# Two mixture-of-experts layers: every expert on all rows, against blocks of 256 chosen rows

## The chip, the cores and the metric

The kernel runs on one core of one Trainium2 chip. The metric is device microseconds from launch to the last store. Three runs of the kernel before gave 1663.55, 1663.65 and 1663.83 us; the median is 1663.65 us.

## The reference

The input is `x` of 8 sequences of 256 tokens, 256 features each: 2048 rows. Four sublayers follow, each with a residual and a layer norm. All arithmetic is float32.

```python
x = layernorm(x + attention(x))          # 16 heads of 128, causal, 8 sequences
x = layernorm(x + experts0(x))           # 32 experts of width 96, top 6, shared width 192
x = layernorm(x + state_space(x))        # in_proj, conv, 8 heads of decaying attention, out_proj
x = layernorm(x + experts1(x))           # 16 experts of width 176, top 4 of 2 of 4 groups, shared 352

def experts0(x):
    scores = sigmoid(x @ gate_w)
    topk_w, topk_i = top_k(scores, 6)
    topk_w = topk_w / (sum(topk_w) + 1e-20)
    combine = sum(one_hot(topk_i, 32) * topk_w[..., None], axis=1)     # [t, 32], 6 entries not zero
    act = silu(einsum('td,edf->tef', x, wg)) * einsum('td,edf->tef', x, wu)
    routed = einsum('tef,efd,te->td', act, wd, combine)
    return routed + silu(x @ sg) * (x @ su) @ sd
```

`experts1` is of the same kind, with a softmax, and with four entries of sixteen that are not zero. The reference computes every expert for every row, and multiplies most of the results by zero.

## The kernel before

The instruction stream of each engine is written out by hand, in the order in which it runs; semaphores order the engines against each other. The same `for s in range(...)` loop stands in each engine's block, and each says at which step `s` the engine does what. All matrix products in float32 are three products of rounded halves (`passes`: hi x hi, hi x lo, lo x hi), so each tile that a product reads exists as a high part (written by ScalarE) and a low part (written by VectorE or GpSimd).

**Attention** (lines 547 to 1350 in each engine's `group`) runs over 8 groups of two heads, 16 units each. In its shadow the expert weights are split into halves: SyncE loads a tile of `w_all`, ScalarE (`split_high`) and GpSimd (`split_low`) split it, and SyncE stores it in `w_split`, 56 tiles in all.

**The experts, dense.** The hidden columns of all experts are laid side by side and cut in tiles of 128. A step `s` takes one such tile for one quad (512 rows, a quarter of the tokens): `gate_up(s)` on TensorE makes 12 products of 512 columns (gate and up), ScalarE takes the silu (`gate`, L742), VectorE multiplies (`activate`, L1082), GpSimd multiplies by the combine weights of the rows (`combine`, L578), ScalarE and VectorE make the halves (L750, L1088), and `down(s)`, two steps later, makes 12 products of 256 columns. Layer 0 has 2 shared and 24 expert tiles, layer 1 has 3 and 22, each for 4 quads: 204 steps, 184 of them of experts. Combine weights go through DRAM (`comb_store`, `comb_load`) to be repeated over the partitions.

**The state-space sublayer** works on 4 pairs of sequences (512 rows each). It is not a stage of its own: pair `p` is spread over the steps from `FRONT[p]` on (33, 65, 97, 129), some 50 steps long, so that TensorE does expert tiles between its products. Its head loop goes over 8 heads, 2 steps each: VectorE scans decays (L1152), GpSimd multiplies by `gram` (`mixes`, L600), ScalarE makes the high part (L802), GpSimd the low part (`mix_low`, L606), TensorE the products. The norms and gates of the quads are spread in the same way (`NORM0`, `NORM1`).

## Time and profile before

| | |
|---|---|
| median of three runs | 1663.65 us |
| profiled execution, first to last instruction | 1664.1 us |
| TensorE busy | 1607.4 us (97%) |
| VectorE busy | 1131.1 us (68%) |
| ScalarE busy | 764.6 us (46%) |
| GpSimd busy | 628.7 us (38%) |
| DMA | 277.75 MB, mean 167 GB/s |

The page gives the execution that was profiled by its span, 1664.1 us, which lies 0.45 us above the median of the runs; no other time of it is given. "PE" is TensorE, "DVE" VectorE, "ACT" ScalarE, "POOL" GpSimd, "SP" SyncE, which issues all DMAs of the kernel before. Busy time of TensorE has overlaps in it: the records of two products that follow each other overlap, so the distance of two starts, not the duration, is what a product costs. The first expert product starts at 611.4 us; what is before it is attention, what is behind it are the 204 steps with everything else between them. The last 9 us are the last quad's norm and store.

### The profile page before, as it was taken

The page shows a single profiled execution, that of the slowest core. Times are in us where ns is not written, and L with a number is a line of the kernel's source. Part 1 is how long each engine was busy: PE and PEld are TensorE (multiplying, and loading weights), DVE is VectorE, ACT ScalarE, POOL GpSimd, SP SyncE. Part 2 cuts the span into 40 slices and gives each one's busy share as a digit, 9 for nine tenths or more (in the row PEclk, how much of TensorE's full clock was granted, in tenths as well). Part 3 has the DMA queues.
Part 4 walks back from the last instruction along what each step waited for, and adds up shares of the span by engine and source line. Part 5 has one row for each costly group of instructions (what it writes and reads, how often), then busy time and mean ns, then how long its engine had stood idle before and what let it go on. Part 6 is the DMA issues. An engine that isn't in the chain of part 4 may idle for free.

```text
span 1664.1 us, 29632 instructions
## 1 busy us (share of the span) xinstructions
PE 1607.4 (97%) x9944; PEld 1403.7 (84%) x9944; DVE 1131.1 (68%) x2877; ACT 764.6 (46%) x1889; POOL 628.7 (38%) x379
## 2 busy tenths in 40 slices
PE   7999999999999979999999999999999999999997
PEld 6988888898888868888888888888888888888886
DVE  5878878787887765556467568748784867753533
ACT  5666656666665543434433443325333533323221
POOL 2322223232222004323377335841575147533242
PEclk9999999999999999999999999999999999999999
DMA  6444335343443016666676556655655466555563
GB/s 212 159 140 143 141 118 180 132 158 139 142 141 137 1 59 205 191 196 205 199 225 188 184 176 209 194 187 165 207 189 175 146 206 197 178 175 172 195 206 107
DMA packets 101241, 277.75 MB, mean 167 GB/s; under 512 B 13488, under 2 KB 17584, under 8 KB 100112
## 3 DMA queue, kind: packets, MB, share of 16 engines
q1 hardware_dynamic: 101136, 276.39, 51.6%
q8 instruction: 61, 1.00, 0.2%
q14 instruction: 44, 0.36, 0.1%
HBM read 229.18 MB, written 46.63 MB: 166 GB/s over the span
## 4 chain that ended last, share of the span: by engine, by line
PE 60%; issue 14%; DVE 13%; POOL 6%; ACT 4%; DMA 1%; SPq 1%; POOLq 0%; DVEq 0%; ACTq 0%
PE psum L352 54%; POOL act_sb L578 4%; PE psum L1324 2%; DVE s_sb L1019 1%; PE psum L1335 1%; PE psum L1514 1%; POOL mix L600 1%; ACT p_sb L701 1%; PE psum L1314 1%; ACT kT_hi L660 1%; DVE s_sb L1017 1%; DVE kT_lo L913 1%; DVE pT_lo L1034 1%; DVE x L934 1%; DVE p_sb L1027 1%
## 5 line engine op out<-in xcount | busy, mean ns | idle before, releaser
L352 PE MATMUL psum<-xT_hi,gu_w 128*128 128x512 f32 x1616 | 550.3, 401 | 4.2 <-DVE act_sb L1082 4.0
L578 POOL TENSOR_TENSOR act_sb<-act_sb,comb 128x512 f32<-128x512 f32 x184 | 311.1, 1691 | 614.8 <-DVE act_sb L1082 614.6
L1082 DVE TENSOR_TENSOR act_sb<-psum,gated 128x512 f32<-128x512 f32 x204 | 140.7, 690 | 378.9 <-PE psum L352 372.6
L742 ACT ACTIVATE gated<-psum 128x512 f32<-128x512 f32 x204 | 122.2, 599 | 600.3 <-PE psum L352 597.8
L352 PEld LDWEIGHTS psum<-xT_hi,gu_w 128*128 128x128 f32 x1616 | 304.2, 188 | 78.0 <-DVE act_sb L1082 5.6
L352 PE MATMUL psum<-xT_lo,gu_w 128*128 128x512 f32 x808 | 319.6, 395 | 0.0
L352 PEld LDWEIGHTS psum<-d_w,act_hi 128*128 128x128 f32 x1632 | 221.5, 188 | 19.7 <-issue 2.1
L544 POOL TENSOR_TENSOR split_stage<-raw_stage,split_stage 128x768 fp32r<-128x768 f32 x56 | 103.1, 1840 | 354.2 <-ACT split_stage L650 354.2
L352 PE MATMUL psum<-d_w,act_hi 128*128 128x256 f32 x1632 | 227.7, 282 | 0.4 <-ACT act_hi L750 0.4
L352 PEld LDWEIGHTS psum<-xT_lo,gu_w 128*128 128x128 f32 x808 | 152.2, 188 | 28.8
L1088 DVE TENSOR_TENSOR act_lo<-act_sb,act_hi 128x512 fp32r<-128x512 f32 x204 | 148.8, 729 | 2.1 <-ACT act_hi L750 1.8
L750 ACT ACTIVATE act_hi<-act_sb 128x512 fp32r<-128x512 f32 x204 | 127.3, 624 | 17.1 <-POOL act_sb L578 16.9
L699 ACT ACTIVATE p_sb<-s_sb,neg_max 128x128 f32<-128x128 f32 x128 | 51.5, 403 | 172.0 <-DVE neg_max L1019 172.0
L352 PE MATMUL psum<-d_w,act_lo 128*128 128x256 f32 x816 | 130.1, 282 | 0.0
L352 PE MATMUL psum<-xT_hi,aw_hi 128*128 128x512 f32 x256 | 104.1, 407 | 9.9 <-POOL aw_lo L540 9.9
L352 PEld LDWEIGHTS psum<-d_w,act_lo 128*128 128x128 f32 x816 | 111.2, 188 | 0.0
L352 PE MATMUL psum<-xT_hi,aw_lo 128*128 128x512 f32 x256 | 102.1, 399 | 0.0
L352 PE MATMUL psum<-xT_lo,aw_hi 128*128 128x512 f32 x256 | 101.8, 398 | 0.0
L600 POOL TENSOR_TENSOR mix<-mix,gram 128x768 f32<-128x768 f32 x32 | 94.3, 2947 | 0.0
L1026 DVE TENSOR_SCALAR p_sb<-p_sb,row_inv 128x128 f32<-128x128 f32 x128 | 83.1, 649 | 4.6
L352 PE MATMUL psum<-aw_hi,xT_hi 128*128 128x256 f32 x256 | 74.7, 292 | 9.7 <-DVE kT_lo L913 8.3
L352 PE MATMUL psum<-aw_hi,zT_hi 128*128 128x256 f32 x256 | 80.5, 315 | 2.5 <-DVE zT_lo L1039 2.5
(203 smaller groups left out, 3473.6 us busy)
## 6 DMA issues: line engine op xcount, KB each, us to landing
gu_w<-w_split SPq DMA_DIRECT2D x204, 512.0 KB, 3.6
d_w<-w_split SPq DMA_DIRECT2D x204, 256.0 KB, 3.8
w_split<-split_stage SPq DMA_DIRECT2D x56, 768.0 KB, 3.9
raw_stage<-w_all SPq DMA_DIRECT2D x56, 384.0 KB, 4.3
decay_all<-decay_dram SPq DMA_DIRECT2D x32, 384.0 KB, 5.3
in_w<-w_split SPq DMA_DIRECT2D x40, 256.0 KB, 4.1
aw_raw<-attn_w SPq DMA_DIRECT2D x8, 1024.0 KB, 6.3
comb<-l_comb_dram SPq DMA_DIRECT2D x128, 64.0 KB, 3.1
```

The source lines that it names most:

```text
L352: last = nc.tensor.matmul(out_ap, w, m, start=start and n == 0, stop=stop and n == len(pairs) - 1, **kw)
L544: pool.tensor_tensor(split_stage[:, k % 2, :, 1, :], raw_stage[:, k % 2, :].rearrange("p (j w) -> p j w", j=3), split_stage[:, k % 2, :, 0 ...
L578: pool.tensor_tensor(act_sb[:, s % 2, :], act_sb[:, s % 2, :], comb[:, comb_block(s) % 2, :], ALU.mult).then_inc(comb_done, 1)
L600: pool.tensor_tensor(mix[:, g % MIXES], mix[:, g % MIXES], gram[:], ALU.mult).then_inc(mix_ready, 1)
L660: act.activation(kT_hi[:, bp % 2, j // 2, :], bank, ACT.Copy).then_inc(qkv_hi, 1)
L699: act.activation(p_sb[:, u % 3, 0:P], s_sb[:, u % 2, 0:P], ACT.Exp, bias=neg_max[:, u % 3, 0:1], scale=-1.0, accum_out=row_sum[:, u % 3, 0:1])
L742: act.activation(gated[to, s % 2, :], psum[0:to.stop - to.start, G_BANK, :], ACT.Silu).then_inc(gated_ready, 1)
L750: act.activation(act_hi[rows_of(s), s % 2, :], act_sb[rows_of(s), s % 2, :], ACT.Copy).then_inc(act_hi_ready, 1)
L1026: dve.tensor_scalar(p_sb[:, u % 3, 0:P], p_sb[:, u % 3, 0:P], row_inv[:, u % 3, 0:1], None, ALU.mult)
L1082: dve.tensor_tensor(act_sb[r, s % 2, :], psum[r, G_BANK if packed(s) else U_BANK, :], gated[r, s % 2, :], ALU.mult).then_inc(t_ready, 1)
L1088: dve.tensor_tensor(act_lo[r, s % 2, :], act_sb[r, s % 2, :], act_hi[r, s % 2, :].bitcast(F32), ALU.subtract).then_inc(act_lo_ready, 1)
L1324: last = pe.transpose(psum[:, PT_BANK, i * P:(i + 1) * P], p_sb[:, u % 3, i * P:(i + 1) * P], ident[:])
```

## The change

The expert layers become sparse. `choose` and `slots` on VectorE and `rank` on TensorE (two products with a triangle of ones) number the rows of each expert. For each expert there is a region of 2048 rows in DRAM (`xs`); GpSimd writes each row of `x` into the regions of its 6 (or 4) experts with indirect DMAs, 128 rows of 1 KB each (`scatter`). `table` computes where blocks of 256 rows begin; the number of blocks is fixed by the worst case, 79 in layer 0 and 47 in layer 1, and blocks that no expert needs take rows of zeros. SyncE reads the address of a block from SBUF into a register, loads its rows and its expert's unsplit weights, and stores the block's result in `os`. After the last block GpSimd gathers the 6 (or 4) result rows of each token with indirect DMAs, and VectorE adds them with their weights (`weights`, `combine`).

The state-space sublayer now stands between the two block loops, over slots `t` of its own, with `FRONT` at 14, 46, 78, 110; of the experts only the 12 shared steps of layer 1 are left in it, with the gathers of layer 0 and the scatters of layer 1. In attention 14 tiles are split in place of 56, and SyncE writes zeros to all 42 regions of `xs` (2 MB each).

```diff
 BLOCK = 256
 REGION = T
+def most_blocks(f):
+    return (T * f["top"] + f["experts"] * (BLOCK - 1)) // BLOCK
-SPLITS = 8
+SPLITS = 2
-FRONT = 33, 65, 97, 129
-NORM0 = None, 1, 10, 19
-NORM1 = 28, 54, 82, 115
+FRONT = 14, 46, 78, 110
+SLOTS = FRONT[-1] + 52
+MIX_AT = {t: t if t < QUAD else FRONT[t // QUAD] - 26 + 4 * (t % QUAD) for t in range(TILES)}
+SHARED_AT = {FRONT[p] + 44 + 2 * j: STEPS0 + p * L1["tiles"] + j for p in range(QUADS) for j in range(L1["tiles"])}
...
         @block.sync
+                for k in range(ZEROED):
+                    n = ZEROED * g + k
...
+                    sp.dma_start(dst.rearrange("p (a w) -> p a w", w=1024), zeros[:].to_broadcast([P, REGION // P * D // 1024, 1024])) \
+                        .then_inc(xs_zeroed, 16)
...
+            def first_row_of(n):
+                f, m = block_of(n)
+                return sp.value_load(rows_at[f["layer"]][m:m + 1, 0:1], min_val=0, max_val=f["last_row"])
+            def block_load(n):
+                f, m = block_of(n)
+                row = first_row_of(n)
+                wait(sp, xb_turned, n - XB_RING + 1)
+                sp.dma_start(xb[:, n % XB_RING], xs[bass.ds(row, BLOCK)].rearrange("(i p) d -> p i d", p=P)).then_inc(xb_loaded[n % XB_RING], 16)
+                wait(sp, bw_lo_ready, n - W_RING + 1)
+                sp.dma_start(bw_raw[:, n % W_RING, 0:f["cols"]],
+                             expert_w[f["layer"]][bass.ds(row >> 11, 1)].rearrange("a p w -> p (a w)")).then_inc(bw_loaded[n % W_RING], 16)
+            def block_store(n):
+                _, m = block_of(n)
+                sp.wait_ge(b_copied, n + 1)
+                sp.dma_start(os[m * BLOCK:(m + 1) * BLOCK].rearrange("(i p) d -> p i d", p=P), b_out[:, n % OUT_RING]).then_inc(b_stored[n % OUT_RING], 16)
+            def blocks(f):
+                first = FIRST[f["layer"]]
+                sp.wait_ge(rows_known, f["layer"] + 1)
+                for q in range(QUADS):
+                    sp.wait_ge(scattered[q], 16 * QUAD * (L0["top"] + f["layer"] * L1["top"]))
+                for n in range(first, first + 2):
+                    block_load(n)
+                for n in range(first, first + f["blocks"]):
+                    if n + 2 < first + f["blocks"]:
+                        block_load(n + 2)
+                    if n > first:
+                        block_store(n - 1)
+                block_store(first + f["blocks"] - 1)
...
         @block.gpsimd
-            def combine(s):
-                pool.wait_ge(t_ready, s + 1)
-                pool.wait_ge(comb_loaded[comb_block(s) % 2], comb_landed(comb_block(s)))
-                pool.tensor_tensor(act_sb[:, s % 2, :], act_sb[:, s % 2, :], comb[:, comb_block(s) % 2, :], ALU.mult).then_inc(comb_done, 1)
+            def scatter(f, q):
...
+                pool.wait_ge(placed, QUADS * f["layer"] + q + 1)
+                for t in range(QUAD * q, QUAD * (q + 1)):
+                    for k in range(f["top"]):
+                        pool.indirect_dma_start(xs, bass.IndirectOffsetOnAxis(ap=row_of[:, t, k:k + 1], axis=0), x[:, t, :], None) \
+                            .then_inc(scattered[q], 16)
+            def block_low(n):
...
+                pool.tensor_tensor(bw_lo[:, n % W_RING, w], bw_raw[:, n % W_RING, w], bw_hi[:, n % W_RING, w].bitcast(F32), ALU.subtract).then_inc(bw_lo_ready, 1)
+            def gather(f, t):
+                i = f["layer"] * TILES + t
+                wait(pool, combined, i - MIX_RING + 1)
+                for k in range(f["top"]):
+                    pool.indirect_dma_start(og[:, i % MIX_RING, k, :], None, os,
+                                            bass.IndirectOffsetOnAxis(ap=back_of[f["layer"]][:, t, k:k + 1], axis=0)).then_inc(og_loaded[i % MIX_RING], 16)
...
         @block.tensor
+            def blocks(f):
+                first, end = FIRST[f["layer"]], FIRST[f["layer"]] + f["blocks"]
+                for n in range(first, first + 2):
+                    block_turn(n)
+                block_gate_up(first)
+                for n in range(first, end):
+                    if n + 2 < end:
+                        block_turn(n + 2)
+                    if n + 1 < end:
+                        block_gate_up(n + 1)
+                    block_down(n)
```

`block_turn` makes four transposes of 128x128; `block_gate_up` makes 12 products of 256 columns in layer 0 and 18 in layer 1; `block_down` 6 and 12. Around them ScalarE makes the high parts of the rows (`block_turned`, 512 elements a partition) and of the weights (`block_high`, 640 or 1280), the silu and the high part of the activation; VectorE the low parts, the product and the copy of the result out of PSUM (`block_copy`); GpSimd the low part of the weights (`block_low`).

On GpSimd, just behind attention, before: `combine` of the first expert tiles (`act_sb` is the activation, `comb` the weights of the rows).

```order
L578 TENSOR_TENSOR act_sb<-act_sb,comb 128x512 [waits comb_loaded1,t_ready] x3
L578 TENSOR_TENSOR act_sb<-act_sb,comb 128x512 [waits comb_loaded0,t_ready] x2
L590 TENSOR_TENSOR ow_lo<-ow_raw,ow_hi 128x1024 [waits ow_hi_done]
L578 TENSOR_TENSOR act_sb<-act_sb,comb 128x512 [waits comb_loaded0,t_ready]
L578 TENSOR_TENSOR act_sb<-act_sb,comb 128x512 [waits comb_loaded1,t_ready] x3
```

The same place of the changed kernel, up to the first gathers (`xs` the regions, `row_of` the addresses, `og` the gathered rows, `os` the results):

```order
L674 DMA xs<-x,row_of 86016x256 [waits placed,xs_zeroed]
L674 DMA xs<-x,row_of 86016x256 x23
L700 MEMSET start_row 128x128 [waits o_added]
L702 COPY start_row<-ident 128x128 x2
...
L674 DMA xs<-x,row_of 86016x256 [waits placed]
L674 DMA xs<-x,row_of 86016x256 x23
L681 TENSOR_TENSOR bw_lo<-bw_raw,bw_hi 128x640 [waits bw_hi_ready] x79
L688 DMA og<-os,l_back_of 128x256 [waits weighed,b_stored2,ow_split,b_stored1,b_stored0]
L688 DMA og<-os,l_back_of 128x256 x11
```

The multiplications by the weights are gone from GpSimd's stream, and 96 indirect DMAs stand in it ahead of the first block.

On SyncE's queue, before, the loads of two expert tiles in layer 0:

```order
L439 DMA gu_w<-w_split 128x1024 [waits u_ready]
L444 DMA d_w<-w_split 128x512 [waits down_done]
L460 DMA comb<-l_comb_dram 32x512 [waits comb_stored,comb_done]
L460 DMA comb<-l_comb_dram 32x512 x3
L439 DMA gu_w<-w_split 128x1024 [waits u_ready]
```

After, one block of layer 0 (`xb` its rows, `bw_raw` its weights, `b_out` its result), and the beginning of the next:

```order
L518 TENSOR_LOAD l_rows_at
L518 ISA x2
L524 ISA [waits xb_turned]
L524 DMA xb<-xs 128x2x256
L526 ISA [waits bw_lo_ready]
L526 DMA bw_raw<-l_w 128x640
L532 DMA os<-b_out 128x2x256 [waits b_copied]
L518 TENSOR_LOAD l_rows_at
```

The load of a block's rows now stands behind the store of the block four before it, which waits for its copy out of PSUM.

On GpSimd, in the head loop of pair 1, after (`mix` the decays of a head, `og` the gathers for pair 2, `xs` the scatter of pair 0 for layer 1):

```order
L688 DMA og<-os,l_back_of 128x256 [waits combined]
L688 DMA og<-os,l_back_of 128x256 x5
L711 TENSOR_TENSOR h_lo<-h_tok,h_hi 128x512 [waits h_hi_ready]
L723 TENSOR_TENSOR mix_lo<-mix,mix_hi 128x512 [waits mix_hi_ready]
L717 TENSOR_TENSOR mix<-mix,gram 128x768 [waits gram_copied,since_ready]
...
L674 DMA xs<-x,row_of 86016x256 [waits placed]
L674 DMA xs<-x,row_of 86016x256 x15
L717 TENSOR_TENSOR mix<-mix,gram 128x768 [waits gram_copied,since_ready]
```

Before, an expert's `combine` stands in most of these places; now indirect DMAs do.

## Rows read from the trace of the kernel before

**Rows 1.** The page: busy time by engine, and the chain's shares by engine.

```profile
PE 1607.4 (97%) x9944; PEld 1403.7 (84%) x9944; DVE 1131.1 (68%) x2877; ACT 764.6 (46%) x1889; POOL 628.7 (38%) x379
...
PE 60%; issue 14%; DVE 13%; POOL 6%; ACT 4%; DMA 1%; SPq 1%; POOLq 0%; DVEq 0%; ACTq 0%
```

**Rows 2.** Windows of the span: start:end, length, busy us by engine, clock, DMA share, GB/s.

```profile
300.00:400.00 100.00, 95.61 (x669) 86.16 (x668) 79.36 (x256) 62.61 (x206) 26.26 (x16) 1.00 0.37 130
...
560.00:600.00 40.00, 33.84 (x240) 30.55 (x238) 30.49 (x123) 19.00 (x74) 0.00 (x0) 0.96 0.00 1
...
1000.00:1100.00 100.00, 98.53 (x573) 83.56 (x572) 70.78 (x129) 36.47 (x63) 68.74 (x37) 1.00 0.63 195
```

**Rows 3.** Timeline, 1640 to 1664 us: start us, us, engine, line, operation.

```profile
1643.19 0.60 ACT L742 ACTIVATE gated<-psum 128x512 f32<-128x512 f32 x1 [3.10 <-PE psum L352]
...
1647.43 0.60 ACT L742 ACTIVATE gated<-psum 128x512 f32<-128x512 f32 x1 [3.12 <-PE psum L352]
...
1648.63 1.11 PE L352 MATMUL psum<-d_w,act_hi 128*128 128x256 f32 x8
...
1649.58 0.63 PE L352 MATMUL psum<-d_w,act_lo 128*128 128x256 f32 x4
...
1655.09 1.40 DVE L920 BATCH_NORM_STATS2 stats<-x 128x6 f32<-128x256 f32 x4
...
1659.33 1.38 DVE L934 TENSOR_SCALAR x<-x,mv,rstd 128x256 f32<-128x256 f32 x4
```

**Rows 4.** The chain of waits, 540 to 620 us: start us, us, what.

```profile
591.62 0.87 PE psum L1357 x8
...
611.40 5.19 PE psum L352 x18
```

**Rows 5.** Windows of 5 us around the end of attention.

```profile
585.00:590.00 5.00, 3.96 (x21) 3.99 (x22) 3.76 (x14) 2.18 (x9) 0.00 (x0) 0.66 0.00 0
...
605.00:610.00 5.00, 2.34 (x17) 1.93 (x16) 3.71 (x21) 2.37 (x4) 0.00 (x0) 1.00 0.00 0
610.00:615.00 5.00, 4.63 (x16) 3.66 (x17) 1.57 (x3) 0.60 (x1) 0.00 (x0) 0.66 0.09 21
...
625.00:630.00 5.00, 5.00 (x29) 4.09 (x28) 4.41 (x12) 1.32 (x3) 1.67 (x1) 1.00 0.89 302
```

**Rows 6.** Timeline of SyncE's queue, 1000 to 1012 us.

```profile
1006.90 0.35 SPq L439 DMA_DIRECT2D gu_w<-w_split  x1
```

**Rows 7.** DMA issues of the page: KB each, median us from issue to landing.

```profile
gu_w<-w_split SPq DMA_DIRECT2D x204, 512.0 KB, 3.6
d_w<-w_split SPq DMA_DIRECT2D x204, 256.0 KB, 3.8
...
aw_raw<-attn_w SPq DMA_DIRECT2D x8, 1024.0 KB, 6.3
```

**Rows 8.** Groups of GpSimd over the whole span: mean ns of one behind the busy us.

```profile
L600 POOL TENSOR_TENSOR mix<-mix,gram 128x768 f32<-128x768 f32 x32 | 94.3, 2947 | 0.0
L606 POOL TENSOR_TENSOR mix_lo<-mix,mix_hi 128x512 fp32r<-128x512 f32 x32 | 49.3, 1540 | 11.5 <-ACT mix_hi L802 11.5
...
L590 POOL TENSOR_TENSOR ow_lo<-ow_raw,ow_hi 128x1024 fp32r<-128x1024 f32 x1 | 2.4, 2394 | 0.0
```

**Rows 9.** Groups of VectorE and ScalarE by form, 600 to 1664 us.

```profile
L1088 DVE TENSOR_TENSOR act_lo<-act_sb,act_hi 128x512 fp32r<-128x512 f32 x200 | 146.0, 730 | 2.0 <-ACT act_hi L750 1.8
...
L750 ACT ACTIVATE act_hi<-act_sb 128x512 fp32r<-128x512 f32 x200 | 124.8, 624 | 17.0 <-POOL act_sb L578 16.9
...
L1152 DVE TENSOR_TENSOR_SCAN mix<-decay_all,start_row 128x768 f32<-128x768 f32 x32 | 82.5, 2579 | 0.1
...
L1129 DVE SCALAR_TENSOR_TENSOR conv<-psum,cols,conv 128x508 f32<-128x508 f32 x20 | 14.9, 747 | 0.7
```

**Rows 10.** Timeline of GpSimd, 780 to 960 us, two of the eight mixes of a pair.

```profile
853.87 3.29 POOL L600 TENSOR_TENSOR mix<-mix,gram 128x768 f32<-128x768 f32 x1
...
861.58 1.85 POOL L600 TENSOR_TENSOR mix<-mix,gram 128x768 f32<-128x768 f32 x1
```

985 lines of the change are left out of this document (637 added, 348 removed).

## The prediction

> **What bounds the kernel now.** I read the page first: TensorE is busy 97% of the span and holds 60% of the chain that ended last [rows 1]. The windows say where the others stand: in attention and in the experts TensorE leaves under 5 us of 100 open, and only in the last group of attention, 560 to 600 us, does it fall to 33.8 of 40 [rows 2]. The timeline of the last tiles gives the price of an expert step: the silus of two steps start at 1643.19 and 1647.43, 4.24 us apart. Eight products of 256 columns start at 1648.63 and the next at 1649.58, so one costs 0.119 us, and one of 512 columns (4.24 - 12 x 0.119) / 12 = 0.234 us [rows 3]. Attention ends and the first step begins at 611.4 us; eight transposes of 128x128 take 0.87 us, 0.11 each [rows 4]. So 1053 us lie behind attention, of which 204 x 4.24 = 865 are expert steps; the other 188 are products of the state-space sublayer, gates and the end. VectorE (70.8 of 100) and GpSimd (68.7 in the head loop of a pair) work beside that.
>
> **What goes.** 184 steps of experts, 184 x 4.24 = 780 us of TensorE. What comes in their place on TensorE: a block of layer 0 has 18 products and 4 transposes, 18 x 0.119 + 0.44 = 2.6 us, 79 of them 204 us; one of layer 1 has 30, 4.0 us, 47 of them 188 us. TensorE alone saves 388 us, and if it stayed the bound the kernel would take 1276 us. It doesn't stay the bound: rows must be scattered before the first block, blocks have a chain of loads, and the state-space sublayer loses the steps that hid it.
>
> **1. Attention, 611 to 616 us.** Fewer tiles are split (14 for 56), but TensorE is the bound there and gains little: 5 us. Into the last group, where VectorE is busy 30.5 of 40 us [rows 2], go two more norms (a norm from statistics to the scaled rows is 1655.09 to 1660.71, 5.6 us [rows 3]), a second quad's halves and the numbering: 20 us on an engine that is waited for, of which I count half. The 84 MB of zeros are 12.6 MB a group of 68 us; DMA moved 302 GB/s where it was most pressed [rows 5], so 42 us, hidden.
>
> **2. Scatter of layer 0, to 729 us.** 96 indirect DMAs on GpSimd, and SyncE waits for all before it loads a block. No row shows an indirect DMA. Below, it costs as much as an issue by SyncE, 0.35 us [rows 6]; above, as a DMA from issue to landing, 3.8 us for 256 KB [rows 7], if each waited for the one before. GpSimd has to read 128 addresses and write as many descriptors, about the work of a pass over 128x512 (0.00233 us an element by L590, 2394 ns for 1024: 1.2 us) [rows 8]. I take 1.2 and keep 0.35 and 2.0. GpSimd starts with quad 0 at about 608, in attention's last group, is never without work after (quads 2 and 3 are numbered by 660), and needs 96 x 1.2 = 115 us and 4 for constants and `ow_lo`; with 2 us to land 729. The eight shared steps, 8 x 4.24 = 34 us, and the gates lie beside it. This is 113 us in which TensorE mostly idles.
>
> The Trainium skill (DMA: Bandwidth & Descriptors, Specifications) puts the first byte of a DMA issued by GpSimd at about 1 us. If that were GpSimd's own time for one, the sum would be 50 us lower, since some 250 of the 320 are on the path. No run here shows it.
>
> **3. Blocks of layer 0, 79 x 4.3 us.** TensorE's 2.6 us and DMA's 852 KB at 302 GB/s, 2.8 us, are both under the chain that I find: copy of block n-2 out of PSUM (0.7, as any pass of VectorE over 128x512, L1088 [rows 9]), store issue 0.35, the address into a register (no row; 0.1 to 2, I take 0.6), landing of the rows 3.8 [rows 7], transposes 0.44, 12 products 1.4, 6 products 0.7, four handoffs of 0.1 (semaphores; an estimate) = 8.4 us for two blocks and a little for loads that meet stores, 8.6, 4.3 each. The loads of block n+2 stand behind the store of n-2 on SyncE's queue, hence two. 79 x 4.3 = 340, and 10 to fill the pipe: 1079 us. ScalarE (0.62 for 512 elements, 0.75 for 640, two of 0.37 [rows 9]: 2.1), VectorE (2.2) and GpSimd (640 x 0.00233 = 1.5) hide under it. Bounds: 3.6, by the chain through the weights (10.8 us for three blocks), and 5.6, if TensorE runs at its lower clock.
>
> **4. The state-space sublayer, bare: 529 us.** Before, a pair took 32 steps of 5.2 us, 166 us, and hid. Now it runs at its own pace. Head loop: GpSimd does 8 x (2.95 + 1.54) [rows 8] and waits 0.7 us eight times for ScalarE's high part: 41.5 us; `h_lo` and `square_add` 6; for the middle pairs one gather of 6 and the scatter of 16, 22 x 1.2 = 26: 73 us (54 for the first, 66 for the last). The other half of a pair is VectorE's: 15 taps of 0.75 (11), `h_tok`, dt and decays (6), a norm (6), combining (6 DMAs' rows a tile, 12 x 0.5 = 6), outputs (2), with the handoffs of five convolution jobs between TensorE, ScalarE and VectorE: 39 us. Four loops and three halves: 54 + 73 + 73 + 66 + 3 x 39 = 383. Ahead of the first loop: 24 gathers (29), norm (5.6), turns (3.4), and the first half with the round trip of the decays (45): 83. Behind the last: output, norm 5.6, gate, scatter 19, together 63. 1079 + 529 = 1608 us. Bounds of a period of 112 us: VectorE's own sum, 88 (8 scans of 2.58 [rows 9] 21, taps 11, two norms 11, outputs 13, combining 12, gate and numbering 12, shared steps 4, the rest 4), and 150 with costlier indirect DMAs.
>
> GpSimd and VectorE disturb each other: the same multiplication takes 3.29 us at 853.87 and 1.85 at 861.58 [rows 10]. The Trainium skill (SBUF — State Buffer, "SBUF: two separate sides") says that the two share a port pair under an exclusive lock, and that descriptors written by GpSimd wait for it. By the mean of 2.95 the loop costs as above; by 1.85 it would be 9 us shorter a pair. By that rule the trace agrees for ordinary passes; for descriptors no run here shows it, and it is a rival below.
>
> **5. Blocks of layer 1, 47 x 5.5 us.** The rows' chain gives 0.7 + 0.35 + 0.6 + 3.8 + 0.44 + 2.1 + 1.4 + 0.4 = 9.8 for two. The weights' is longer: copy, store, address and two issues 2.3, landing of 655 KB about 5 (between 3.6 for 512 and 6.3 for 1024 KB [rows 7]), ScalarE 1280 elements 1.35, GpSimd 1280 x 0.00233 = 3.0, products 3.5, handoffs 0.6: 15.8 for three blocks, 5.3; with GpSimd at the disturbed rate (3.29 / 768 an element: 5.5 us) 6.1. I take 5.5: 258 us and 10 to fill, 1876 us.
>
> **6. The end: 95 us.** Last store 4 [rows 7], then 64 gathers x 1.2 = 77, landing 2, combining 2, norm 5.6, store 4. In all 1971 us, against a span of 1664.1; the median of the runs lies 0.45 us under the span, so I forecast 1970 us.
>
> **Rivals.** (a) *Faster: every unknown is at its cheap end.* An indirect DMA is 0.35 us, so that the numbering of quads 2 and 3 ends the scatter, about 660; blocks take 3.6 and 4.9 us, 294 + 240; a pair takes VectorE's 88, four of them and 60 around, 412; the end 38: 660 + 294 + 412 + 240 + 38 = 1644 us. For it: VectorE and GpSimd have 30% and more open today; against it: all must hold at once, and each chain has waits that I rather missed than counted double. With cheap indirect DMAs alone it is 1971 - 250 x 0.85 = 1760, still slower. It decides where the period falls under 90 us and a block under 4.
>
> (b) *Indirect DMAs at 2 us or more*, because VectorE holds the port or descriptors are slow: 250 x 0.8 = 200 us more, 2170. For it [rows 10], against it that VectorE is nearly idle in the scatter and at the end.
>
> (c) *The clock falls.* The granted clock fell to 0.66 over 585 to 590 and 610 to 615 us [rows 5], which is part of the time at 1.2 GHz for 2.4; before the second TensorE had been busy 2.3 of 5 us. In the blocks it would be busy 60 to 70%. At the lower clock all through, blocks cost 1.3 us more in layer 0 and 2 in layer 1: 103 + 94, 2170 us; half of that is more likely, 2070.
>
> (d) *Sparse, but not by as much as it says.* The rows need 12288 / 256 = 48 full blocks and some 16 for ragged ends in layer 0, 32 and 8 in layer 1; 79 and 47 are run whatever the routing. The 22 spare blocks, 15 x 4.3 + 7 x 5.5 = 103 us, are in the sum already.
>
> **Chances.** The sum as it stands, 1860 to 2060 us: 0.53. Dear indirect DMAs or a low clock, above 2060: 0.15. Cheap indirect DMAs or a shorter period, 1670 to 1860: 0.16. Rival (a), under 1660: 0.15, since its terms go together more than their number suggests (one cost of an indirect DMA stands in four of them). Within 3 us of the kernel before: 0.01. A measurement of this kernel can tell 0.2%, 3 us, from no change. Faster 0.15, the same 0.01, slower 0.84. The range is 1720 to 2140; left out of it are rival (a) and the far ends of (b) and (c), about 0.2; the likeliest's own is 1860 to 2060.
>
> **What would show it.** TensorE's busy share falls to about 65%, with a hole between attention and the first block of about 100 us in which GpSimd issues 96 DMAs (step 2); TensorE's transposes of a block wait for the DMA of its rows, 4.3 us apart (3), and in layer 1 its products for `bw_lo` (5); the first scans of two pairs' head loops lie 112 us apart (4); 77 us of gathers at the end (6). Wrong would be: indirect DMAs that leave GpSimd in well under 1 us, blocks under 4 us, or a period near VectorE's own sum.

## The result, and the profile after

The changed kernel takes 2090.11 us (median of four runs, 2081.31 to 2093.60), the kernel before 1663.70 beside it: a ratio of 1.2545, interval 1.2523 to 1.2567. The sparse kernel is 426 us slower. The prediction was 1970 us in a range of 1720 to 2140, with 0.84 on slower. In a later set of runs, told below, the same kernel took 2140.69 us, while the kernel before stayed at 1664.

The profiled execution spans 2091.5 us. The page's busy time by engine and the chain's shares answer to [rows 1]:

```profile
PE 1465.0 (70%) x8868; PEld 1268.9 (61%) x8868; DVE 1296.1 (62%) x3449; ACT 816.7 (39%) x2016; POOL 788.1 (38%) x607
...
PE 21%; DVE 16%; POOL 13%; issue 10%; DMA 7%; ACT 3%; SPq 2%; DVEq 0%; POOLq 0%; ACTq 0%
```

TensorE went from 97% of the span to 70%, and from 60% of the chain to 21%. GpSimd, which held 6% of the chain, holds 13%, and DMA went from 1% to 7%. No engine bounds the whole kernel; in most of it chains through several of them do. The windows tell it by stage, as [rows 2] before: scatter, blocks of layer 0, the state-space sublayer, blocks of layer 1, the end. Columns: stretch, length, busy us of PE, PEld, DVE, ACT, POOL, clock, DMA share, GB/s.

```profile
610.00:738.00 128.00, 56.33 (x249) 45.43 (x248) 43.77 (x166) 19.51 (x31) 96.90 (x104) 0.67 0.41 140
752.00:1110.00 358.00, 254.79 (x1694) 242.28 (x1692) 203.89 (x394) 146.94 (x306) 117.70 (x76) 0.85 0.55 181
1187.00:1603.00 416.00, 230.70 (x1060) 179.18 (x1060) 289.75 (x574) 123.38 (x185) 235.13 (x184) 0.72 0.33 105
1703.00:1989.00 286.00, 270.61 (x1534) 218.01 (x1533) 176.70 (x322) 137.56 (x222) 128.62 (x44) 0.93 0.53 181
1989.00:2091.00 102.00, 0.09 (x1) 0.00 (x0) 52.62 (x161) 0.00 (x0) 61.18 (x64) 0.50 0.35 106
```

Only in the blocks of layer 1 is TensorE nearly full (271 of 286 us). In the scatter it is busy 56 of 128, in the state-space sublayer 231 of 416, at the end not at all.

The indirect DMA, which no row of before showed, on GpSimd's timeline (start, us, engine, line, operation, idle before it), and its groups over the span (busy us, mean ns):

```profile
613.34 0.96 POOL L674 DMA_INDIRECT xs<-x,row_of  x1 [0.31 <-issue]
614.61 0.96 POOL L674 DMA_INDIRECT xs<-x,row_of  x1 [0.30 <-issue]
615.87 0.96 POOL L674 DMA_INDIRECT xs<-x,row_of  x1 [0.31 <-issue]
```

```profile
L674 POOL DMA_INDIRECT xs<-x,row_of x160 | 159.6, 998 | 166.7 <-DVE row_of L1190 119.5
...
L688 POOL DMA_INDIRECT og<-os,l_back_of x160 | 159.4, 996 | 125.7 <-DVE x L1253 60.0
```

An indirect DMA is 0.96 us on GpSimd and 0.30 before the next, 1.265 us from start to start. Its data lands 2.4 us (scatter) or 2.7 us (gather) after the issue, by the median. The forecast took 1.2 us for one.

One block of layer 0 in the middle of its stage, SyncE's queue and VectorE's copies out of PSUM (which answer to the steps of the chain in step 3):

```profile
902.97 0.37 SPq L532 DMA_DIRECT2D os<-b_out  x1
904.10 0.37 SPq L524 DMA_DIRECT2D xb<-xs  x1
...
908.79 0.37 SPq L532 DMA_DIRECT2D os<-b_out  x1
```

```profile
898.90 0.68 DVE L1291 COPY b_out<-psum 128x512 f32<-128x512 f32 x1
...
902.26 0.68 DVE L1291 COPY b_out<-psum 128x512 f32<-128x512 f32 x1
...
908.08 0.68 DVE L1291 COPY b_out<-psum 128x512 f32<-128x512 f32 x1
...
911.31 0.68 DVE L1291 COPY b_out<-psum 128x512 f32<-128x512 f32 x1
```

The copy of 902.26 is followed by its store at 902.97, and only then by the load of the rows for the block four behind it, at 904.10. Copies are 3.4 and 5.8 us apart by turns, two blocks in 9.2 us, and every load stands behind a store, in the pattern that the forecast drew. From the end of the store's issue (903.34) to the load's issue 0.76 us pass, in which SyncE fetches the address. Landings and zeros, from the page (KB each, median us from issue to landing), answer to [rows 7]:

```profile
xs<-zeros SPq DMA_DIRECT2D x42, 2048.0 KB, 22.3
xb<-xs SPq DMA_DIRECT2D x126, 256.0 KB, 2.7
...
bw_raw<-l_w SPq DMA_DIRECT2D x47, 640.0 KB, 4.0
```

And GpSimd's passes over the state-space stretch answer to [rows 8]: the mix is cheaper, 1.96 us for 2.95 on the mean.

```profile
L717 POOL TENSOR_TENSOR mix<-mix,gram 128x768 f32<-128x768 f32 x32 | 62.8, 1963 | 25.2 <-DVE mix L1454 25.2
L723 POOL TENSOR_TENSOR mix_lo<-mix,mix_hi 128x512 fp32r<-128x512 f32 x32 | 46.2, 1444 | 51.9 <-ACT mix_hi L978 51.9
```

VectorE is as busy beside it as before (290 of 416 us, 70%, against 70.8 of 100), so it is not that. What went is the meeting of two instructions. Before, 24 of the 32 mixes ran beside a scan of VectorE, and each of them took 3.3 us; seven of the other eight took 1.83 to 1.85. In the changed kernel three of 32 meet a scan, and one of these takes 3.26 us; the 29 others take 1.8 to 2.3. One pair before, and the dear one after:

```profile
852.69 2.83 DVE L1152 TENSOR_TENSOR_SCAN mix<-decay_all,start_row 128x768 f32<-128x768 f32 x1
853.87 3.29 POOL L600 TENSOR_TENSOR mix<-mix,gram 128x768 f32<-128x768 f32 x1
```

```profile
1601.14 2.83 DVE L1454 TENSOR_TENSOR_SCAN mix<-decay_all,start_row 128x768 f32<-128x768 f32 x1
1602.31 3.26 POOL L717 TENSOR_TENSOR mix<-mix,gram 128x768 f32<-128x768 f32 x1
```

In stages, against the forecast. The marks are those of the forecast's steps: the first load of layer 0's blocks (738), the first gather (1112), the first load of layer 1's blocks, which follows the last scatter (1682), and the last store (1990).

| stage | forecast | measured |
|---|---|---|
| scatter, to the first block's load | 729 | 738 |
| blocks of layer 0 | 350 | 374 |
| state-space sublayer | 529 | 570 |
| blocks of layer 1 | 268 | 308 |
| end | 95 | 101.5 |
| sum | 1971 | 2091.5 |

### The profile page after: what moved, and what is told of

The parts are those of the page before. It is cut to its first block, busy times and chain, and to the rows that moved or that the text cites. A ratio compares the mean times of both kernels' runs of the same rounds, so it can differ in the third digit from the quotient of the medians.

```text
span 2091.5 us, 28959 instructions
## 1 busy us (share of the span) xinstructions
PE 1465.0 (70%) x8868; PEld 1268.9 (61%) x8868; DVE 1296.1 (62%) x3449; ACT 816.7 (39%) x2016; POOL 788.1 (38%) x607
## 4 chain that ended last, share of the span: by engine, by line
PE 21%; DVE 16%; POOL 13%; issue 10%; DMA 7%; ACT 3%; SPq 2%; DVEq 0%; POOLq 0%; ACTq 0%
PE psum L397 16%; POOL xs L674 7%; DMA xb<-xs 5%; POOL og L688 4%; PE psum L1870 2%; DVE conv L1431 2%; DVE x L1253 2%; DVE b_out L1291 2%; DMA bw_raw<-l_w 1%; SPq L518 1%; DVE mix L1454 1%; DVE stats L1100 1%; DVE x L1114 1%; DVE act_sb L1275 1%; ACT act_hi L919 1%
## 5 line engine op out<-in xcount | busy, mean ns | idle before, releaser
L681 POOL TENSOR_TENSOR bw_lo<-bw_raw,bw_hi 128x640 fp32r<-128x640 f32 (+1 forms) x126 | 259.7, 2061 | 409.8 <-ACT bw_hi L900 409.8
L674 POOL DMA_INDIRECT xs<-x,row_of x160 | 159.6, 998 | 166.7 <-DVE row_of L1190 119.5
L397 PE MATMUL psum<-xbT_hi,bw_hi 128*96 128x256 f32 (+1 forms) x598 | 200.5, 335 | 27.8 <-DVE xbT_lo L1262 19.1
L688 POOL DMA_INDIRECT og<-os,l_back_of x160 | 159.4, 996 | 125.7 <-DVE x L1253 60.0
L397 PE MATMUL psum<-xbT_hi,bw_lo 128*96 128x256 f32 (+1 forms) x598 | 188.9, 316 | 0.0
L397 PE MATMUL psum<-xbT_lo,bw_hi 128*96 128x256 f32 (+1 forms) x598 | 188.7, 316 | 0.0
L900 ACT ACTIVATE bw_hi<-bw_raw 128x640 fp32r<-128x640 f32 (+1 forms) x126 | 117.3, 931 | 108.0 <-DMA bw_raw<-l_w 107.8
L1262 DVE TENSOR_TENSOR xbT_lo<-psum,xbT_hi 128x512 fp32r<-128x512 f32 x126 | 86.8, 689 | 101.5 <-ACT xbT_hi L893 93.0
L397 PEld LDWEIGHTS psum<-xbT_hi,bw_hi 128*96 128x96 f32 (+1 forms) x598 | 123.4, 206 | 32.6 <-DVE xbT_lo L1262 21.0
L824 ACT ACTIVATE p_sb<-s_sb,neg_max 128x128 f32<-128x128 f32 x128 | 51.5, 402 | 195.5 <-DVE neg_max L1320 195.5
L397 PEld LDWEIGHTS psum<-xbT_lo,bw_hi 128*96 128x96 f32 (+1 forms) x598 | 124.0, 207 | 0.0
L397 PEld LDWEIGHTS psum<-xbT_hi,bw_lo 128*96 128x96 f32 (+1 forms) x598 | 123.8, 207 | 0.0
## 6 DMA issues: line engine op xcount, KB each, us to landing
xs<-zeros SPq DMA_DIRECT2D x42, 2048.0 KB, 22.3
```

Source lines behind the costliest of these rows:

```text
L397: last = nc.tensor.matmul(out_ap, w, m, start=start and n == 0, stop=stop and n == len(pairs) - 1, **kw)
L674: pool.indirect_dma_start(xs, bass.IndirectOffsetOnAxis(ap=row_of[:, t, k:k + 1], axis=0), x[:, t, :], None) \
L681: pool.tensor_tensor(bw_lo[:, n % W_RING, w], bw_raw[:, n % W_RING, w], bw_hi[:, n % W_RING, w].bitcast(F32), ALU.subtract).then_inc(bw_lo ...
L688: pool.indirect_dma_start(og[:, i % MIX_RING, k, :], None, os, bass.IndirectOffsetOnAxis(ap=back_of[f["layer"]][:, t, k:k + 1], axis=0)).t ...
L824: act.activation(p_sb[:, u % 3, 0:P], s_sb[:, u % 2, 0:P], ACT.Exp, bias=neg_max[:, u % 3, 0:1], scale=-1.0, accum_out=row_sum[:, u % 3, 0:1])
L900: act.activation(bw_hi[:, n % W_RING, w], bw_raw[:, n % W_RING, w], ACT.Copy).then_inc(bw_hi_ready, 1)
```

## The experiments

In what follows I divide a run by four marks in its trace: the first and the last copy of a block's result in layer 0, and the same in layer 1. In the changed kernel they stand at 752.4, 1109.7, 1703.2 and 1989.1 us. The marks are those of the one execution that was profiled, which can lie some us beside the median in the second column (e2_fit's by 5.5, e4_half's by 4.0). Times are medians of four executions; the kernel before took 1665.0 us beside the first four, 1665.7 beside the second, 1664.04 beside the last three.

| kernel | median us | ratio, interval | first copy | layer 0 | between | layer 1 | end |
|---|---|---|---|---|---|---|---|
| changed | 2090.1 | 1.2545 [1.2523, 1.2567] | 752.4 | 357.3 | 593.5 | 285.9 | 102.4 |
| e1_ahead | 1992.2 | 1.1963 [1.1944, 1.1983] | 751.3 | 271.1 | 592.4 | 272.3 | 102.5 |
| e2_fit | 1985.7 | 1.1927 [1.1907, 1.1947] | 750.4 | 294.1 | 593.8 | 238.2 | 101.9 |
| e4_half | 1959.4 | 1.177 [1.175, 1.179] | 702.3 | 360.2 | 533.3 | 279.7 | 78.2 |
| e5_weights | 2076.6 | 1.2464 [1.2443, 1.2484] | 773.1 | 345.0 | 593.6 | 262.7 | 102.5 |
| e6_fill_ssm | 2207.6 | 1.327 [1.3239, 1.3301] | 785.5 | 353.3 | 671.8 | 283.2 | 107.6 |
| e6b_fill4 | 2160.5 | 1.298 [1.2959, 1.3002] | 787.0 | 359.0 | 620.1 | 280.7 | 107.4 |
| e7_fill_blocks | 2140.7 | 1.2865 [1.2825, 1.2905] | 788.5 | 348.6 | 609.5 | 279.6 | 107.3 |
| e8_all | 1943.0 | 1.1676 [1.1654, 1.1697] | 811.0 | 195.5 | 611.5 | 213.8 | 106.7 |
| e10_same | 2140.7 | 1.2855 [1.2833, 1.2876] | 785.3 | 356.9 | 606.1 | 287.2 | 107.5 |
| e11_paced | 2137.6 | 1.2846 [1.2824, 1.2867] | 777.7 | 356.3 | 606.9 | 285.9 | 107.5 |
| e12_all | 1941.6 | 1.1674 [1.1649, 1.1699] | 788.6 | 223.9 | 608.7 | 211.3 | 107.3 |

**e1_ahead: loads three blocks ahead.**

```diff
-                for n in range(first, first + 2):
+                for n in range(first, first + 3):
...
-                    if n + 2 < first + f["blocks"]:
-                        block_load(n + 2)
+                    if n + 3 < first + f["blocks"]:
+                        block_load(n + 3)
```

> The changed kernel ran at 2090 us. SyncE loads the rows and weights of a block three blocks ahead instead of two, in the same rings of three; nothing else changes. Theory (chain of loads): the copy of a block, its store, the address, the landing of rows, transposes and products close a ring over two blocks of layer 0 (3.1 and 6 us in turn, 4.3 on average); over three blocks the same chain gives (8.6 + 2.6) / 3 = 3.7 us, and in layer 1 the weights' chain goes from 5.6 to about 5.0: 79 x 0.6 + 47 x 0.6 = 75 us less, 2015 us. Rival (the clock): TensorE's products at the lower clock set the pace, so the wait for rows goes but the blocks stay at 4.3: under 15 us less. If closing the gaps also brings the clock back, layer 0 goes below 3.7 and the time below 2000.

98 us less: 86 in layer 0, where a block falls from 4.58 to 3.48 us, and 14 in layer 1. TensorE's waits for the rows in the blocks of layer 0, the changed kernel (755 to 1108 us) and this run (755 to 1020), and then this run's window (of a wait: us in total, times, longest):

```profile
PE psum L1870 <- DMA xb<-xs: 91.2, 51, 2.8
```

```profile
PE psum L1870 <- DMA xb<-xs: 14.2, 23, 1.9
```

```profile
755.00:1020.00 265.00, 219.32 (x1649) 204.71 (x1648) 192.29 (x384) 145.77 (x300) 116.43 (x75) 0.94 0.73 240
```

The wait of the transposes for the rows was 91.2 us in 51 places and is 14.2 in 23. This shows step 3's chain: nothing was changed but the place of the loads in SyncE's queue. The clock of the stretch rose from 0.85 to 0.94 with it, and layer 0 fell below the 3.7 us a block of the chain alone; that the clock accounts for the rest fits what was expected, but no run parts the two. In layer 1 the gain is half of what was expected.

**e2_fit: as many blocks as the routing needs.** For this input 64 blocks in layer 0 and 40 in layer 1 are enough.

```diff
-    _l["blocks"] = most_blocks(_l)
+    _l["blocks"] = (64, 40)[_l["layer"]]
```

> The loops run 64 and 40 blocks, what the routing of this input needs, instead of 79 and 47. A block dropped is worth what a block costs. Theory: 15 x 4.4 + 7 x 5.7 = 106 us less, 1984 us. Rival: spare blocks, whose rows are zeros and lie together, are cheaper than others, under 70 us less.

104 us less by the medians. In the profiled executions it is 63 in layer 0 for 15 blocks (4.2 us each) and 48 in layer 1 for 7 (6.8); that this is more than 104 is the spread of single executions. Rival (d) was in the sum with 103 us.

**e4_half: half of the indirect DMAs.** Each row is scattered to half of its experts only, and half of the result rows are gathered and used twice; the result is not the reference's.

```diff
-                    for k in range(f["top"]):
+                    for k in range(f["top"] // 2):
                         pool.indirect_dma_start(xs, ...
...
-                for k in range(f["top"]):
+                for k in range(f["top"] // 2):
                     pool.indirect_dma_start(og[:, i % MIX_RING, k, :], ...
```

> Half of the indirect DMAs are left out, in scatters and gathers (a row goes to three of its six experts, or two of four, and each gathered row is used twice); all other work stays. 160 fewer at 1.265 us from start to start. Theory: about 250 of 320 are on the path (scatter of layer 0, front of the state-space stage, the middle of its pairs, last scatter, end), so 125 x 1.265 = 158 us less, 1932 us. Rival: within the pairs of the state-space stage VectorE and the handoffs set the pace, so only scatter (48), front (12), last scatter (8) and end (32) count: 100 x 1.265 = 126 us less, 1964 us. If the numbering of rows on VectorE takes over in the scatter, less than 100 us.

131 us less for 160 indirect DMAs. The first copy comes 50 us earlier for 48 of them, 1.04 us each; the end is 24 us shorter for 32 and the stretch between the layers 60 us shorter for 80, 0.75 us each. In the scatter they cost most of their 1.265 us: 48 of them are 61 us, of which GpSimd gave 12 back, since it now waited 4.8 us ahead of `ow_lo` and 7.1 us for the numbers of a quad. Between the layers and at the end two fifths hide.

The theory, with 125 of the 160 on the path at the full price, expected 158 us and falls. The rival's 126 us was near, but not for its reasons: it had 40 us at the end and 25 between the layers, where 24 and 60 were measured. Within the pairs of the state-space stage they do cost, as the theory had it (57 us).

**e5_weights: the weights of the rows before the blocks.** `weights` is VectorE's work for the gather; the change put it behind blocks 4, 6, 8 and 10 of each layer.

```diff
-                    for q in range(QUADS):
-                        if n == first + 4 + 2 * q:
-                            weights(f, q)
...
+            for q in range(QUADS):
+                weights(L0, q)
             blocks(L0)
```

and the same behind `table(L1)`.

> VectorE computes the combine weights of the four quads before the first block (beside the scatters) instead of behind blocks 4, 6, 8 and 10 of each layer, where two blocks took 12.9 us instead of 9. Theory: that time was on the path, 4 x 3.9 us in layer 0 and about 4 x 4.5 in layer 1, and goes: 33 us less, 2057 us (a few us less of gain if layer 1's last scatter is too short to hide them). Rival: the blocks behind would have made it up, under 8 us less.

14 us less (13.5 by the medians), by three parts that the marks show: the blocks of layer 0 take 12 us less and begin 21 later, since the work now stands between the last scatter and the first block; the blocks of layer 1 take 23 less and the stretch before them is the same (593.6 for 593.5), so there it is hidden. The term of 35 us is real, and only in layer 1 did this place hide it.

**e6_fill_ssm and e6b_fill4: products that nobody reads, in the state-space stage.** The same edit with 8 and with 4, in the 150 slots that have no shared step:

```diff
...
+                if t not in SHARED_AT:
+                    if t - 1 in SHARED_AT:
+                        pe.wait_ge(gated_ready, started)
+                    for _ in range(8):
+                        pe.matmul(psum[:, G_BANK, :], ow_hi[:, 0, 0:P], ow_hi[:, 2:4, :].rearrange("p j d -> p (j d)"), start=True, stop=True)
```

> Eight products of 512 columns that nobody reads (ow_hi with itself, into the bank of the state-space stage's gate) are added on TensorE in each of some 150 slots between the two block loops; all else is as in the changed kernel. At 0.234 us each that is 281 us of the 594 between the layers' copies. Theory (GpSimd and VectorE set the pace there, TensorE's low clock of 0.57 to 0.74 is what its idleness brings and costs little): the clock of the stage rises above 0.85, and the time stays at 2090 within 15 us. Rival (the low clock is where the 58 us went that the stage took over my forecast): 2030 to 2060 us. Third: the added products do not fit in the idle time, and TensorE becomes the bound: above 2120 us.

> The same with four products a slot, 140 us at full clock. Theory: the clock of the stage rises by less, to about 0.8, and the time stays at 2090 within 10 us. Rival (the low clock costs): 2040 to 2070 us. If eight make the kernel slower and four do not, it is the room on TensorE and not the waits around the products.

These runs began the blocks 33 us later, a difference that is not theirs (e10_same, below). Against e10_same they take 67 and 20 us more, and 66 and 14 of these lie between the layers. Against e7_fill_blocks, which ran beside them and leaves this stretch as it was (609.5 us), it is 62 and 11. The state-space stretch of the run with eight and of the one with four:

```profile
1210.00:1700.00 490.00, 405.58 (x1996) 325.68 (x1996) 308.54 (x605) 140.62 (x207) 239.29 (x187) 0.92 0.29 94
```

```profile
1210.00:1650.00 440.00, 316.21 (x1504) 249.16 (x1502) 299.61 (x600) 136.87 (x200) 224.16 (x179) 0.84 0.33 104
```

The clock rose to 0.92 and 0.84 from 0.72, and neither run got faster: the rival falls as a remedy. But the theory of enough idle time was wrong too. With 140 us of added products the stage grows by 14 and with 281 by 66, although TensorE stays idle for 124 and 84 us of these stretches. My reading is that its idle time is cut into waits in a chain in which TensorE takes part, so that an added product delays what comes next; no run tests this apart. Nor can these runs say how much the low clock costs by itself, since they change two things.

**e7_fill_blocks: such products in the wait for rows.** They stand ahead of the transposes of 77 of the 79 blocks.

```diff
...
+                        pe.wait_ge(xb_lo_ready, n + 1)
+                        for _ in range(4 if f["layer"] == 0 else 0):
+                            pe.matmul(psum[:, turn_bank(n + 2), :], ow_hi[:, 0, 0:P], ow_hi[:, 2:4, :].rearrange("p j d -> p (j d)"), start=True, stop=True)
                         block_turn(n + 2)
```

> Four products of 512 columns that nobody reads are added ahead of the transposes of each block of layer 0, where TensorE waits for the rows: 0.94 us a block at full clock, 74 us. Theory (the rows' chain through SyncE's queue sets the 9 us of two blocks, and the clock of 0.85 there is a consequence): one of the two fillings of a pair lies in the wait and the other delays by 0.94 us, of which the clock gives a part back, so 2090 to 2125 us, with the clock above 0.95. Rival (the low clock is the cause of the 9 us): 2050 us or less, because 36 products of a pair at 0.119 instead of 0.14 us and faster transposes win 1 us a block.

The time is that of e10_same (2140.74 and 2140.69). The 250 us from 850 on, this run and then the unchanged one, and the waits for the rows over the blocks of layer 0 (790 to 1137 and 790 to 1140), in the same order:

```profile
850.00:1100.00 250.00, 210.66 (x1494) 184.06 (x1493) 140.76 (x233) 110.19 (x231) 89.03 (x57) 1.00 0.60 196
```

```profile
850.00:1100.00 250.00, 175.30 (x1238) 166.73 (x1237) 131.83 (x226) 108.41 (x225) 86.59 (x56) 0.90 0.58 192
```

```profile
PE psum L1870 <- DMA xb<-xs: 52.6, 47, 2.8
```

```profile
PE psum L1870 <- DMA xb<-xs: 101.1, 54, 4.4
```

With 77 x 4 x 0.234 = 72 us of added products the clock stands at 1.00 instead of 0.90 and TensorE is busy 35 us more of 250. About half of the wait for the rows is filled, and the layer takes 348.6 us for e10_same's 356.9; the two other runs of this set that leave these blocks alone took 353.3 and 359.0. So in this layer the added work cost nothing, and what the full clock gave back beyond it is 5 to 10 us, in single executions. The total stands at the low end of the theory's 0 to 35 us more, with the clock above the 0.95 that it named. The rival's 40 us less is refuted: the clock is a small part of the 9 us of two blocks.

**e8_all: three edits.** Those of e1_ahead and e2_fit, and `weights` of layer 1 behind its table, of layer 0 at `f == 8` of the shared steps:

```diff
+                if f == 8:
+                    for q in range(QUADS):
+                        weights(L0, q)
```

> Three edits together: rows and weights loaded three blocks ahead, 64 and 40 blocks for 79 and 47, and the weights of the rows computed ahead of the blocks, in layer 0 now in the hole in which VectorE waits for the scatter. From the traces: first copy of a block at 751; 64 blocks at 3.26 us (271.1 us of the run with three ahead less 17 for the weights, over 78), 209; 593 between the layers; 40 blocks at 5.41, 216; end 102: 1868 us. If the three do not add, since with rows early another engine is next, 1890 to 1910 us. In no case does it reach 1664: 593 us between the layers and 138 of scatter and pipe are left.

1943 us, 75 above the sum, of which the 50 us of e10_same (below) are not the edits'. The blocks do what was expected and better (195.5 and 213.8 us). What failed lies ahead of and between them: the first copy at 811.0, some 23 us behind the runs beside it, and 611.5 us between the layers, as in e7_fill_blocks. `weights` sits there from 771.8 to 797.1 us, in front of the first block and not in the hole, since VectorE came to it only when ScalarE's `gated` was there, after a wait of 39.9 us. That wait led to the next runs.

**e10_same: the changed kernel again.** No edit.

> The changed kernel, unchanged, beside the next two. In the runs with added products the first block's copy came at 786 to 788 us instead of 751 to 752 although nothing ahead of it differs, the stretch between the layers was 16 us longer where nothing in it differs, and the end 5 us longer; TensorE, ScalarE, VectorE and SyncE stood still for 10 to 25 us at a time with no releaser while GpSimd issued indirect DMAs at its constant 1.265 us. If the kernel's time depends on the chip or the moment, this gives either about 2090 or 2140 to 2150 us; if the code's layout did it, 2090 us wherever it runs.

2140.69 us, interval of the ratio 1.2833 to 1.2876, where the first result had 1.2523 to 1.2567, and 1664.04 for the kernel before. The program is the same to the letter, so the layout of the code falls as a cause. The three sets of experiments ran on three chips. The first set has the marks of the kernel's first result, the other two the later ones. So the time of this kernel differs by 2.4% from one set to another, that of the one before by 0.1%. The chip is the likely cause; but none is known to have been used at two times, so the chip and the moment aren't parted. 33 us of the 50 lie ahead of the first copy, 13 between the layers, 5 at the end: the stretches with indirect DMAs. The blocks take the same (357 and 287). ScalarE's waits between 612 and 770 us ("remote" is a releaser that the trace doesn't show):

```profile
ACT gated L868 <- remote: 81.1, 3, 47.8
ACT xT_hi L802 <- remote: 26.3, 3, 9.9
ACT gated L868 <- issue: 17.4, 2, 14.5
```

In the changed kernel's own trace the same silu of 25.36 us' wait looks like this, and then in e10_same:

```profile
625.52 0.59 ACT L868 ACTIVATE gated<-psum 64x512 f32<-64x512 f32 x1 [2.86 <-PE psum L397]
```

```profile
649.76 0.59 ACT L868 ACTIVATE gated<-psum 64x512 f32<-64x512 f32 x1 [25.36 <-remote]
```

2.86 us behind TensorE in the first, 25.36 behind nothing that is shown in the other; GpSimd's indirect DMAs run on meanwhile at 1.265 us. All six kernels of the two later sets that have no gap between the DMAs show this wait for the same silu, 24.5 to 26.7 us; all four of the first set have 2.7 to 3.3 us there, behind TensorE. The gate's numbers for quads 2 and 3 come late, and GpSimd itself, which had been without a gap in the first trace, waits:

```profile
693.17 2.39 POOL L707 TENSOR_TENSOR ow_lo<-ow_raw,ow_hi 128x1024 fp32r<-128x1024 f32 x1 [20.87 <-ACT ow_hi L877]
702.61 1.10 POOL L674 DMA_INDIRECT xs<-x,row_of  x1 [7.05 <-DVE row_of L1190]
```

20.87 and 7.05 us, 28 together: most of the 33. The rest lies behind the last scatter: the last silu of the shared steps stood 47.76 us until 768.59, past the scatter's end, and GpSimd's first pass over weights waits 13.0 us for ScalarE instead of 7.0.

**e11_paced: gaps in the scatter of layer 0.**

```diff
                     for k in range(f["top"]):
                         pool.indirect_dma_start(xs, ...
+                    if f["layer"] == 0:
+                        pool.wait_ge(scattered[q], 16 * f["top"] * (t - QUAD * q + 1))
```

> In the scatter of layer 0 GpSimd waits behind the six indirect DMAs of each 128 rows until they have landed: 16 waits of about 2.4 us, 38 us. Theory (the other engines stand still because indirect DMAs follow each other without a gap): their waits without a releaser between 612 and 738 us (TensorE 25.4 us at the longest in the changed kernel) fall under 10 us, and numbering and shared steps are done earlier; the scatter ends 38 us later, 2128 us if the unchanged kernel takes 2090, and about the same as the unchanged one where that takes 2140. Rival (they have another cause): the waits stay as long, and the time is 38 us above the unchanged kernel's wherever it runs.

On the same chip as e10_same, 2137.58 and 2140.69 us: intervals of the ratios that overlap, though 16 waits for landings were added. That is what the theory expected where the unchanged kernel takes 2140 us; the rival's 38 us more did not come. ScalarE in the same places, waits and the same silu:

```profile
ACT gated L870 <- PE psum L397: 50.8, 6, 28.8
ACT logitT L810 <- issue: 10.9, 2, 6.9
...
ACT xT_hi L804 <- remote: 2.0, 1, 2.0
```

```profile
625.60 0.59 ACT L870 ACTIVATE gated<-psum 64x512 f32<-64x512 f32 x1 [2.97 <-PE psum L397]
```

ScalarE's waits with no releaser were 81.1 + 26.3 + 17.4 us and are 14; the 25.36 us are 2.97. The numbers of quads 2 and 3 are ready when GpSimd comes to them (`ow_lo` at 688.68 instead of 693.17, the next scatter at 691.19 instead of 702.61), and the first copy is 8 us earlier in spite of the waits. The stretches whose DMAs were left without gaps are as long as in e10_same (606.9 and 107.5 us). So ScalarE's standstill goes with indirect DMAs that follow each other without a gap: on one chip it is there without the gaps and gone with them. For TensorE this isn't shown. The expectation was that all such waits fall under 10 us, and its longest without a releaser grew, from 15.3 to 23.2 us (25.4 in the changed kernel's first trace). What is held up, and why the same run of DMAs did not hold up ScalarE in the first set, is not settled.

**e12_all: three edits, layer 0's weights left in place.** e1_ahead, e2_fit and `weights(L1, q)` behind `table(L1)`.

> Rows and weights loaded three blocks ahead, 64 and 40 blocks for 79 and 47, and the weights of the rows computed ahead of the blocks in layer 1 only. Where the unchanged kernel takes 2090 us: first copy at 751, blocks of layer 0 271 less 15 x 3.26 = 222, 593 between the layers, 40 blocks of layer 1 216, end 102: 1884 us, 206 below the unchanged kernel of the same chip. If computing all weights ahead of the blocks was what cost the run of three edits its time (first copy at 811 us, 23 later than the runs beside it), this one is 5 to 10 us faster than that one's 1943 at the same pace of the chip; if not, slower by up to 12.

1941.62 us, 199 below the unchanged kernel on its chip, against 206 expected. It was expected to be 5 to 10 us faster than e8_all if the weights ahead of the blocks were what cost that one its time, and up to 12 slower if not; 1.4 us faster is neither. The 22 us that it saves ahead of the first copy it gives back in the blocks of layer 0 (223.9 for 195.5). The two are the fastest versions that compute everything, and still 17% slower than the kernel before, though they already know the number of blocks. Its stretch between the layers (608.7), what is ahead of the first copy (788.6) and the end (107.3) are 1505 us by themselves. With the 751, 593 and 102 us of the first set it would be 1446, and the 218 us left to reach 1664 are half of what the blocks take.

## Why the prediction was right, and where it was 120 us short

**Right in direction, and in the mechanism but for layer 1's blocks.** TensorE loses its place as the bound, and three things that it used to hide come bare, in the order of the forecast: GpSimd's row by row scatter (step 2: 729 forecast, 738 measured), the state-space sublayer at its own pace (4) and the gathers at the end (6: 95 and 101.5). The 1.2 us of an indirect DMA was worked out from a GpSimd pass over 128x512; it is 1.265, and the bounds of 0.35 and 2.0 were both far off. That a pass of like size has the price of an indirect DMA was a guess that came out. The 0.065 us over the 250 on the path are 16 us. The time lies in the range, but above the likeliest part, where the forecast had put 0.15 on dear indirect DMAs or a low clock. Dear DMAs it was not.

**Step 1, 616 us.** The first product of the shared steps starts at 620.2 us, where the first expert product started at 611 before. GpSimd's scatter, which begins at 610.6 and needs no shared step, did not wait for it.

**Step 3, 350 us, measured 374.** The chain is the one forecast: two blocks in about 9 us, 8.6 in the sum, and e1_ahead breaks it by moving the load. Its rows land in 2.7 us instead of 3.8. Its address takes 0.76 instead of 0.6, and TensorE at its lower clock takes more (products 0.21 apart instead of 0.119 in one block of the two around 903 us, at a granted clock of 0.51), so the parts miss by turns and nearly cancel. Without `weights`, e5_weights gives 345.0 / 78 = 4.42 us a block for the 4.3 of the step, 9 us in all. Missed was `weights` (12 us), which stood in the diff and was not counted. The rest, 3 us, is filling and emptying the pipe.

**Step 5, 268 us, measured 308: the number was near, the cause was not.** `weights` is 23 us again. The rate without it is 262.7 / 46 = 5.71 us a block, 5.5 in the sum, and the rest is a longer way from the first load to the first copy, 21 us. The step had the chain of the weights as the bound, with TensorE at 4.0 us a block and its products waiting for `bw_lo`. The trace has no such wait from 1703 to 1989 us, and TensorE is busy 271 of these 286 us. Its products are the bound, because they cost more than the step counted, at the full clock too. Lines of one block's `down` and the transposes behind it, and the window of the same stretch, with its clock of 1.00:

```profile
1905.37 0.28 PE L397 MATMUL psum<-bw_hi,act_hi 128*128 128x256 f32 x1
1905.49 0.28 PE L397 MATMUL psum<-bw_lo,act_hi 128*128 128x256 f32 x1
1905.70 0.38 PE L397 MATMUL psum<-bw_hi,act_hi 64*128 64x256 f32 x1
1905.92 0.28 PE L397 MATMUL psum<-bw_lo,act_hi 64*128 64x256 f32 x1
...
1906.99 1.32 PE L397 MATMUL psum<-bw_hi,act_lo 128*128 128x256 f32 x4
1908.24 0.33 PE L1870 MATMUL psum<-ident,xb 128*128 128x128 f32 x1
```

```profile
1905.40:1908.20 2.80, 2.80 (x14) 1.79 (x12) 1.41 (x3) 1.26 (x3) 2.74 (x1) 1.00 0.82 259
```

The 12 products of `down` take 2.87 us instead of 12 x 0.119 = 1.43: most starts are 0.21 apart, and those of the last four 0.31. With them a block is 5.5 us of TensorE without a gap, and in e1_ahead, where the loads come early, copies of layer 1 stand 5.5 us apart one after the other. In this `down` tiles of 128 and of 64 rows take turns; in layer 0's, where all have 96, starts are 0.12 apart. Whether the turns are the reason no run tests. So the 5.5 us of the step is luck, and the 388 us that TensorE was to save is some 70 too high.

**Step 4, 529 us, measured 570.** The front (83 forecast, 81 measured from the first gather to the first mix) is near. From its first mix to the end of its last `mix_lo`, the head loops of the four pairs take 55, 79, 79 and 68 us for 54, 73, 73 and 66. The other halves between them take 48, 48 and 43 us for 39 each, which is the term that was missed most, and the tail 70 for 63. The first mixes of the pairs stand at 1193.3, 1296.3, 1422.9 and 1544.2 us: periods of 103, 127 and 121 us for 93, 112 and 112. The loops came out near with one part too dear: a mix costs 1.96 us and not 2.95, 8 us a pair, and waits took its place. VectorE is busy 290 of 416 us there, GpSimd 235, TensorE 231, none of them full, and the longest waits go around in a ring (1112 to 1700 us):

```profile
PE psum L397 <- POOL mix_lo L723: 124.8, 17, 22.3
ACT xT_hi L802 <- PE psum L1671: 91.5, 10, 46.6
...
DVE y L1462 <- PE psum L1838: 81.8, 8, 24.1
...
POOL og L688 <- DVE x L1253: 53.8, 3, 24.2
```

TensorE waits for GpSimd, ScalarE and VectorE for TensorE, GpSimd for VectorE. I counted each engine's work along the ring and too few of the handoffs, and TensorE's pieces at the full clock, where 0.72 was granted. e4_half shows that 60 us between the layers go with half of the indirect DMAs; e6b_fill4 that the ring lengthens by 11 to 14 us when TensorE gets 140 us more work. How the 41 us share out between handoffs and clock stays open.

**The rivals.** (a) The cheap indirect DMA is refuted by the first row of GpSimd's timeline. (b) 2 us beside VectorE: the longest scatter took 1.95 us on the engine and the longest gather 2.35, both beside a scan of VectorE (the scans start at 1330.54 and 1187.73 us), but the mean of all is 1.0. The port pair that the Trainium skill (SBUF — State Buffer, "SBUF: two separate sides") has VectorE and GpSimd share: in these runs it cost descriptors little on the mean. (c) The clock is part of it: 0.85 in the blocks of layer 0, 0.72 in the state-space stretch; full clock in e7_fill_blocks was worth 5 to 10 us net of the added work. (d) The spare blocks are measured, 104 us for 103. What no rival had is that the same program takes 50 us more in another set of runs: the price of indirect DMAs is not only GpSimd's, ScalarE can stand still while they run.
